# Comparing the keys of a group of edges one group later, and making a row of numbers ahead of the first gathers

## What is computed

```
def _conv(x, src, dst, Wq, bq, Wk, bk, Wv, bv, Ws, bs):
    q = (x @ Wq + bq).reshape(n, H, HD)
    k = (x @ Wk + bk).reshape(n, H, HD)
    v = (x @ Wv + bv).reshape(n, H, HD)
    alpha = jnp.sum(q[dst] * k[src], axis=-1) / jnp.sqrt(jnp.float32(HD))
    amax = jax.ops.segment_max(alpha, dst, num_segments=n)
    ex = jnp.exp(alpha - amax[dst])
    denom = jax.ops.segment_sum(ex, dst, num_segments=n)
    attn = ex / (denom[dst] + 1e-16)
    msg = v[src] * attn[:, :, None]
    out = jax.ops.segment_sum(msg, dst, num_segments=n).reshape(n, H * HD)
    return out + x @ Ws + bs
```

## Time and profile before

| what | us |
|---|---|
| median of three runs | 4928.97 |
| the profiled execution | 4927.95 |
| its span, first to last instruction | 4926.1 |
| first layer up to the end of `tables` | 153.0 |
| `conv_edges` of the first layer | 153.0 to 744.3 |
| POOL gathers of groups 2 to 12 in it | 232.2 to 686.8 |

### The profile page before, as it was taken

One profiled execution on the slowest core, in us unless ns is written; L12 is line 12 of the kernel. 1 busy time (PEld: TensorE's weight loads), 2 busy tenths in 40 slices (PEclk: granted clock), 3 DMA queues, 4 the chain that ended last, 5 costly groups with the idle time before them and its releaser, 6 DMA issues. The chain is left out here.

```text
span 4926.1 us, 76606 instructions
## 1 busy us (share of the span) xinstructions
PE 3395.7 (69%) x17088; PEld 2562.8 (52%) x17089; DVE 2708.5 (55%) x6617; ACT 1597.4 (32%) x3614; POOL 3350.3 (68%) x3343
## 2 busy tenths in 40 slices
PE   6466766676666666656676688885777756969159
PEld 3366653565535555355564566663767653434124
DVE  7577764666646666556665566655777752111001
ACT  5133332334323333223332355562323312221101
POOL 5177766777767777677776777767777767766720
PEclk6677767778777787777867789895555557989579
DMA  8699946666447675376662766643333202323055
GB/s 262 182 274 273 278 143 183 195 202 204 138 140 217 202 206 158 104 219 203 205 182 83 229 202 202 187 117 86 84 69 82 69 11 91 101 91 97 1 204 198
DMA packets 708257, 784.47 MB, mean 159 GB/s; under 512 B 182494, under 2 KB 585924, under 8 KB 704188
## 3 DMA queue, kind: packets, MB, share of 16 engines
q1 hardware_dynamic: 567932, 478.29, 31.4%
q0 software_dynamic: 139968, 302.44, 22.4%
HBM read 657.83 MB, written 122.47 MB: 158 GB/s over the span
## 5 line engine op out<-in xcount | busy, mean ns | idle before, releaser
L673 POOL DMA_INDIRECT kvconv<-kv_tab,src_all x1664 | 1628.4, 979 | 680.3 <-issue 500.0
L2085 POOL DMA_INDIRECT weights<-of_g,cells_g x416 | 454.8, 1093 | 188.1 <-issue 128.0
L687 POOL DMA_INDIRECT counts<-num_now,ord_now x416 | 432.7, 1040 | 193.1 <-issue 154.1
L673 POOL DMA_INDIRECT rows_r<-rel_tab,idx_r x416 | 421.9, 1014 | 141.1 <-issue 125.0
L673 POOL DMA_INDIRECT kvlast<-kv_tab,src_all x416 | 406.1, 976 | 133.5 <-issue 124.4
L1179 ACT ACTIVATE Sconv<-s8conv 128x512 f32<-128x512 fp8e4 x384 | 240.7, 627 | 354.2 <-PE pA1conv L1135 247.1
L1241 DVE TENSOR_TENSOR msgconv<-kvconv,sm_attEconv 128x512 f32<-128x512 f32 x416 | 285.5, 686 | 83.3 <-PE pA0conv L1135 36.5
L1135 PEld LDWEIGHTS pA0conv<-Sconv,msgconv 128*128 128x128 f32 x1664 | 308.6, 260 | 13.8
L1135 PE MATMUL pA0conv<-Sconv,msgconv 128*128 128x128 f32 x1664 | 308.2, 347 | 0.0
L1169 ACT ACTIVATE STconv<-st8conv 128x512 f32<-128x512 fp8e4 x416 | 257.7, 628 | 106.3 <-DMA st8conv<-st_tab 90.6
L1266 DVE TENSOR_REDUCE sm_alphaconv<-prodbconv 128x16 f32<-128x512 f32 x416 | 283.0, 680 | 2.5 <-DVE sm_exconv L526 0.5
(11 more groups left out here) (634 smaller groups left out, 7853.6 us busy)
## 6 DMA issues: line engine op xcount, KB each, us to landing
qwinconv<-q_tab SPq DMA_DIRECT2D x1664, 64.0 KB
raw_g<-counts SPq DMA_DIRECT2D x50, 896.0 KB, 4.8
hot_g<-weights SPq DMA_DIRECT2D x28, 1600.0 KB, 7.5
weights<-blankconv SPq DMA_DIRECT2D x150, 224.0 KB
kvconv<-kv_tab,src_all POOLq DMA_INDIRECT x1664
st8conv<-st_tab SPq DMA_DIRECT2D x52, 512.0 KB
keyrowconv<-key_tab SPq DMA_DIRECT2D x104, 256.0 KB
s8conv<-s_tab SPq DMA_DIRECT2D x52, 512.0 KB
```

The lines of the kernel that those rows point to most:

```text
L673: nc.gpsimd.indirect_dma_start(rows[:, par * TG + t, :], None, tab, bass.IndirectOffsetOnAxis(ap=idx[:, g * TG + t:g * TG + t + 1], axis=0 ...
L687: nc.gpsimd.indirect_dma_start(counts, bass.IndirectOffsetOnAxis(ap=ord_now[:, i:i + 1], axis=0), num_now[:, i:i + 1], None).then_inc(sem( ...
L2085: nc.gpsimd.indirect_dma_start(weights, bass.IndirectOffsetOnAxis(ap=cells[:, i:i + 1], axis=0), of[:, i:i + 1], None).then_inc(sem("heavy ...
```

## The change

It does five things, all in the first layer. `compare` of a quad moves from its own turn to the turn eight quads later; `matches` from one quad behind to nine; `take` from the group before to the one before that. SP issues key rows 13 quads behind instead of five, so the first one that it issues in the loop stands at quad 15 (1, 7) instead of quad 7 (0, 7), and eight of them stand behind the loop; the weights' columns are loaded at q = 5 for the group before instead of at q = 3. In `tables` POOL makes the numbers before the gathers instead of behind them, and waits first for the copy of what `first_b` held.

```diff
@@ tables, POOL
+                        pool.wait_ge(ch, 1)
+                        nc.gpsimd.iota(first_b[:, :], pattern=[[1, T]], base=V0, channel_multiplier=0).then_inc(placed, 1)
                         for g in range(2):
                             gather_group(pool, "c_", 0, g, g, kv_tab, src_all, kv)
-                        pool.wait_ge(keyed, 1)
-                        nc.gpsimd.iota(first_b[:, :], pattern=[[1, T]], base=V0, channel_multiplier=0).then_inc(placed, 1)
@@ conv_edges, SP, in the loop
                             zeros(g, q)
-                            if marks is not None and not (isinstance(g, int) and g * QG + q < 7):
-                                key_rows(g * QG + q - 5, (q + 1) % 2)
-                            if marks is not None and q == 3 and not (isinstance(g, int) and g < 2):
-                                part_rows(g, par)
+                            if marks is not None and not (isinstance(g, int) and g * QG + q < 15):
+                                key_rows(g * QG + q - 13, (q + 1) % 2)
+                            if marks is not None and q == 5 and not (isinstance(g, int) and g < 3):
+                                part_rows(g - 1, 1 - par)
@@ conv_edges, SP, behind the loop
                     if marks is not None:
-                        for n in range(GROUPS * QG - 5, GROUPS * QG):
+                        for n in range(LAST * QG - 5, LAST * QG):
                             key_rows(n, n % 2)
                     sp.wait_ge(sem(tag + "S"), quad(LAST - 1, 0))
                     settle(sp)
                     sum_rows(LAST, 0)
+                    if marks is not None:
+                        part_rows(LAST, 0)
+                        for n in range(LAST * QG, GROUPS * QG):
+                            key_rows(n, n % 2)
@@ conv_edges, PE
-                            behind = shifted(g, q, par, -1)
+                            behind = shifted(g, q, par, -QG - 1)
@@ conv_edges, DVE
-                        if marks is not None and q == 1 and started(g):
-                            take(g - 1)
+                        if marks is not None and q == 1 and not (isinstance(g, int) and g < 2):
+                            take(g - 2)
...
-                        if marks is not None and scored(g):
-                            compare(g, q)
+                        if marks is not None and started(g):
+                            compare(g - 1, q)
```

## The result

| | us |
|---|---|
| before, median of 8 runs beside it (seven of 4918.97 to 4928.97, one of 10345.03) | 4925.18 |
| after, median of 8 runs (4937.18 to 4945.31) | 4942.92 |
| after / before, 95% interval | 1.0038 [1.0029, 1.0047] |
| after, profiled execution; its span | 4943.74; 4941.9 |

The change costs 0.38%, some 19 us by the ratio (14 to 23), well inside the 2% that I called the measure of no change. The forecast was 4943.0. It is closer than its steps: one term had the wrong sign and was off by 19 us, and what made up for it was in part other terms and in part nothing that I had forecast.

The account below looks back on a forecast made before the run. No engine is full: POOL's gathers pace the middle; the first message and the chain from last `take` over SP to POOL count. Terms -6.3 - 6.5 - 1.5 + 28.5 = +14.2 us gave 4943 us, range 4920 to 4958.

Parts of the forecast that it names:

- Term 1, the iota: In `tables`: with the iota ahead of 64 gathers, DVE's wait for it goes, -6.3 us.
- Term 2, the start: First group of edges: the key-row wait moves from turn 2 to turn 10; first message and gathers come earlier, -6.5 us.
- Term 3, the middle: Gather stretch: the loop's waits stay the same, some POOL stalls may go; -1.5 us, bounds -4.3 and +3.
- Term 4, the end: End of the first layer: last take comes later and SP's writes and POOL's scatters follow unhidden, +28.5 us.
- Waits of the start gone: Rival, first group: the 28.3 us of key-row waits vanish without returning at turn 10, 4921 us; chance 0.16, wholly or half.
- End hidden: Rival, stage's end: POOL's scatters finish beside other work, leaving only the first three terms, 4915 us; chance 0.05.
- The loop slower: Rival, loop: weights' columns come late for `matches`, at most 51 us more, 4994 us; chance 0.09, of which 0.02 beyond 2%.
- Order void: Rival, `tables`: POOL, not DVE, holds its end, so the iota gains nothing, 4949 us; 0.08 together with a longer end.

Follow-up runs that it names:

- e1_iota: The kernel before with only the iota put ahead of the first gathers; ratio 0.9985 to before.
- e2_compare: The kernel after with the iota put back behind the gathers, so only comparisons, takes and key rows are moved; 4951.5 us, 1.0060 of before.
- e3_pad19: The kernel after with 19 one-column memsets in the first block, putting VectorE's loop back at 490; 4921.8 us, 1.0000 of before.
- e6_pad205: The kernel before with 205 one-column memsets in the first block, so VectorE's loop stands at 695; ratio 0.9999 to before.
- e7b_all: The kernel after with 19 one-column memsets (loop at 490) and the first numbers written and read back early; 4894.6 us, 0.9927 of before.
- e4b_early: The kernel after with the number columns of groups 0 and 1 written and the first 60 read back ahead of the last key rows; 4909.7 us, 0.9962 of before.
- e7_all: The kernel after with 19 one-column memsets and early first numbers, run on the slow chip; 6487.3 us, 1.0006 of before there.

## Why the prediction came out, and what in it was wrong

*Term 1, the iota, -6.3.* Right in mechanism: -7.6 in the trace, -7.4 by e1_iota's ratio. Part of the -7.6 is scatter: e2_compare, with the iota in its old place, starts the stage at 151.06, 2.1 us earlier than the kernel before (153.15), and the kernels with the iota ahead start it between 145.38 and 148.45. I called the cover by DVE 2 us thick; it is gone. POOL's last gather ends at 139.9, not 136 (gathers among the last take 4.24, 1.62 and 1.49 us), and POOL sets the end with 0.9 us of wait for DVE. The gain held because POOL needed 5.66 us to close the stage, where I took 8.3 from the scatters of the earlier trace rows.

*Term 2, the start, -6.5.* Right in mechanism, mis-sized: -9.7, within its wide bounds. The wait for a key row does move to turn 10, as a wait of 4.8 us, not over 10. Against the stage's start, SP issued the third key row at 55.7 us, where I had 57.6 (210.6 - 153.04), and its latency was 3.80 us (201.10 to 204.90) instead of 4.6, so the comparison came 9.2 us earlier than before. PE was also later than I allowed: DVE waits 7.4 us for pQ3 and 6.2 for sm_L there, so DVE reached turn 10 late.

*Term 3, the middle, -1.5 with bounds -4.3 and +3.* **This is the step that failed**: +17.7 us, outside its bounds. The sentence "So the loop's waits are the same" was true of semaphores and queues: with the loop's code back in its place, e3_pad19 has 451.4 us, -2.3 against before. What I left out is that taking the comparisons out of the unrolled turns moves the loop's instructions, so that each of its three returns waits for two transfers of instructions: 9.35, 7.57 and 8.17 us. The prediction has no term for it. The three gaps are 25.1 us; POOL's middle grew by 18. That the rows gathered ahead covered the rest is my reading, and no run tests it.

*Term 4, the end, +28.5.* Right: counted from the last gather, the last take came 27.4 us later (38.4 us behind it instead of 11.0) and the next stage's first scatter 26.1. The forecast for PE's first operation of the next stage was 758.5 us. It stands at 770.7 in after, and at 752.6 in e3_pad19, where the three gaps are gone: 18.1 us of the difference are term 3.

*The sum, +14.2.* The four measured terms give +26.5 in this stage, 12.3 more than forecast. The timed difference is only 18.7 us by the ratio and 17.7 by the medians, 8 to 9 less than the terms, and before took 4925.18 beside after, 3.8 less than the 4928.97 to which I had added. That these three cancel, so that 4943 came out to a tenth of a microsecond, is luck. The rest of the program, which is the same source (its instructions stand a little elsewhere in some streams), took from 4167.0 to 4181.1 us in the eight profiled executions of the table, and that of before happens to be the longest. That of e1_iota, whose instructions are the same there as those of before, is 13.0 us shorter. So two profiles can differ by 13 us where nothing was changed, and stage by stage differences are worth more than those of spans. For after, e3_pad19, e6_pad205 and e7b_all the timed result is 8 to 11 us better than the stage's own difference (for e1_iota, e2_compare and e4b_early the two agree within 3.3 us); the cause stays open.

*The rivals.* Waits of the start gone: no; the first message gained 9.7 us, not 28.3. End hidden: no; it could be, but only with another order of writes (e4b_early). The loop slower: yes in kind, for another reason than the late weights' columns: `matches` never waited for them. Order void: no.

## What to carry to other kernels

Taking instructions out ahead of a loop can slow the loop, with every wait and every engine's work unchanged: where a loop body has some hundreds of instructions (311 here), look for "issue" gaps at its first operation and for packets of the instruction queue inside them, and try a few empty instructions ahead of it before judging a reordering. A step that frees one stretch and appends to the stage's last chain pays there in full; ask first which of the chain's data is really needed, since here 60 of 416 columns, taken by 274.2 us and written at 654.7 in e4b_early, took the whole chain off the path. Compare stage by stage, since the unchanged rest scatters by as much as such a change is worth.

## What the hardware showed that was not expected

- A branch back on VectorE, over a body of 311 instructions, cost 7.6 to 9.4 us with the loop at 471 and 3.8 to 5.6 us at 695, and no such gap stood at 490; on the slow chip it was 4.8 to 6.2 us at 471 and 5.0 to 6.3 us at 727. The trace shows the transfers: two packets of instructions in each gap at 471 and 727, one at 695, none at 490.
- Where POOL ends `tables`, DVE starts the next stage 5.66 us after POOL's last gather, the same in five executions; behind the scatters of counts, 9.06 us pass to POOL's next scatter in the seven profiles of these chips where POOL ends the stage (10.81 us in e7b_all, where ACT does).
- On one chip, on two occasions, every kernel took 6389 to 6526 us instead of 4890 to 4956 (but for the one run of 10345.03), with the same program; what is worth 0.7% on another chip (e7b_all) is worth nothing on this one (e7_all). The traces show slower transfers (121 against 159 GB/s) and a lower granted clock (0.68 against 0.74), and don't tell which of them, if either, is the cause.
